# Unread products re-counted, the second tile's rows turned amid the first tile's products, a loaded table for the search, and a quarter of the map's slot columns made by ScalarE

## The chip, the cores and the metric

The kernel runs on one core of one Trainium2 chip. The metric is device time in microseconds (us) of that core. The core's engines run at the same time and meet at semaphores: TensorE (PE: matrix products, with its weight loads, PEld), VectorE (DVE), ScalarE (ACT), GpSimd (POOL, which here issues the indexed transfers) and SyncE (SP, which issues the plain ones); 16 DMA engines move data. All arithmetic here is in fp32, in which TensorE makes each product in two passes, so the profile counts two MATMULs for one call of `matmul` or `transpose`.

## What is computed

Two transformer layers on 4096 tokens (8 batches of 512) of width 256. Each has an attention and then a mixture of 8 experts; layer 0 gives every token to the expert with the highest affinity, layer 1 first lets each expert pick its CAP = 512 most probable tokens.

```python
def _L0_ffn_ref(input_features, centroids, ln_g, ln_b, w1, b1, w2, b2):
    aff = x @ centroids.T
    assign = jnp.argmax(aff, axis=1)
    ...
    for e in range(nE):
        h = _layernorm(xs, ln_g[e], ln_b[e])
        h = jax.nn.relu(h @ w1[e].T + b1[e])
        ye = xs + h @ w2[e].T + b2[e]
        y = y + jnp.where((es == e)[:, None], ye, 0.0)
...
def _L1_ffn_ref(x, Wg, W1, W2):
    probs = jax.nn.softmax(xt @ Wg, axis=-1)
    pT = probs.T
    _, top_idx = jax.lax.top_k(pT, cap)
    sel = jnp.zeros((E, T), dtype=bool).at[jnp.arange(E)[:, None], top_idx].set(True)
    masked = jnp.where(sel, pT, -jnp.inf)
    assigned = sel.any(axis=0)
    tok2exp = jnp.where(assigned, jnp.argmax(masked, axis=0), jnp.argmax(pT, axis=0))
    ...
    for e in range(E):
        gate = jnp.where(tok2exp == e, weights, 0.0)
        h = jax.nn.gelu(xt @ W1[e], approximate=False) @ W2[e]
        out = out + gate[:, None] * h
```

## The kernel before

The program has six stages, one after the other. Layer 0: attention; the plan (which token goes to which slot of which expert's tile); the experts. Layer 1: attention; search and plan; the experts. The order on every engine is the order in which the code is written, and each engine has its own function per stage; semaphores join them.

**The plan.** VectorE picks each token's expert (`choose`), TensorE counts with two products by constant matrices (`prefix_pe`), and VectorE works out each token's slot (`place`, `place_packed`). Then the map from tokens to slots is inverted (`invert_dve`, `invert_pe`). A slot number is split in the place within its tile (`low_f`) and the tile's first slot (`base_f`). For each of the 32 groups of 128 tokens there are 128 columns `low_hot` (is this token's place n?, 128 elements a partition), a row `tile_hot` (which tile?) and `held` = `tile_hot` times (token number, weight). TensorE multiplies `low_hot` by `held` and sums over the 32 groups in one bank (L1049, 64 MATMULs with 78 columns in layer 0 and 68 in layer 1). VectorE makes these operands in four parts of 8 groups (L1030, L1031, L1034) and tells TensorE after each (`p_low`). `keep_tokens` writes the result (L1056, L1057), and with it GpSimd fetches rows tile by tile with indexed transfers (L1173, L1899).

**Unread products.** `hold_clock(eng, n)` (L287) issues n products of the identity with itself into a bank that nobody reads. They stand where TensorE waits for others: 30 ahead of layer 0's map, 25 behind each map ahead of the experts' first rows, 34 ahead of layer 1's map.

**The experts, layer 0** (`expert_stage`, L1136). For each of 39 tiles of 128 rows: `turn_in` transposes the rows (L1198), ScalarE scales them (`act_in`, L1359), `up` makes the hidden layer (L1210, 32 MATMULs) with weights that VectorE has copied (`fetch_weights`, L1297 and L1303), ScalarE makes relu (L1365), `down` multiplies back (L1224), VectorE adds up (`out_rows`), GpSimd stores. There is one bank for turned rows, so `turn_in` of a tile waits until ScalarE has taken those of the tile before. In the steady order TensorE turns tile j, then does `up` of tile j - 1 and `down` of tile j - 2; tile 1 alone is turned behind `up` of tile 0. VectorE and ScalarE wait at the head of the stage for `s_bias`, the four loads that SyncE issues at L1075 to L1078.

**The experts, layer 1** (`f1_tensor` and its fellows, from L1907) have the same order with shorter products (L1916 turns, L1932 up, L1955 down); here too tile 1 is turned behind `up` of tile 0.

**The search** (from L2059) finds each expert's 512th largest probability as a bit pattern, in ROUNDS = 10 rounds of three bits. A round has seven candidates and zero: VectorE counts for the four odd ones how many keys reach them (L2093, with an accumulator read each), ScalarE does so for the three even ones with Sign (L2138) after it has scaled them (`under`, L2135), TensorE sums the counts over the partitions (L2154), and VectorE keeps the largest candidate that at least 512 keys reach (L2097, L2098) and makes the next candidates with the halved steps (L2090, L2095). The steps are built with memsets and shifts at the head of the stage.

## Time and profile before

| | us |
|---|---|
| median of 3 runs | 1015.35 |
| the 3 runs | 1011.42, 1015.35, 1015.40 |
| the profiled execution: its own time | 1017.07 |
| its span | 1015.1 |
| TensorE's mean granted clock, as a share of full speed | 0.975 |
| TensorE busy | 941.4 (93% of the span) |
| VectorE, ScalarE, GpSimd busy | 705.3, 491.7, 321.5 |

Where the stages lie in the span, read from TensorE's timeline: the plan of layer 0 from 205 to 224.7, its experts to 517.5, the attention of layer 1 to 795, search to 829.4, the plan of layer 1 to 861.7, its experts to the end. The times below are us from the span's start. The profiled execution's own time is 1.72 above the median and the three runs differ by 4, which is to be kept in mind where a sum from one trace is set beside the median. Matrix products are pipelined, so that a row's duration of the last one reaches over the next row's start: what a group costs is the distance between starts.

### The profile page before, as it was taken

The page shows a single profiled execution, that of the slowest core. Times are in us where ns is not written, and L with a number is a line of the kernel's source. Part 1 is how long each engine was busy: PE and PEld are TensorE (multiplying, and loading weights), DVE is VectorE, ACT ScalarE, POOL GpSimd, SP SyncE. Part 2 cuts the span into 40 slices and gives each one's busy share as a digit, 9 for nine tenths or more (in the row PEclk, how much of TensorE's full clock was granted, in tenths as well). Part 3 has the DMA queues.
Part 4 walks back from the last instruction along what each step waited for, and adds up shares of the span by engine and source line. Part 5 has one row for each costly group of instructions (what it writes and reads, how often), then busy time and mean ns, then how long its engine had stood idle before and what let it go on. Part 6 is the DMA issues. An engine that isn't in the chain of part 4 may idle for free. (4 is left out here: it accounts for less than half of the span.)

```text
span 1015.1 us, 29867 instructions
## 1 busy us (share of the span) xinstructions
PE 941.4 (93%) x11226; PEld 793.5 (78%) x11227; DVE 705.3 (69%) x1820; ACT 491.7 (48%) x1325; POOL 321.5 (32%) x288
## 2 busy tenths in 40 slices
PE   6899999987999999999999999999878889999996
PEld 3466666887999999999987778888767778888875
DVE  3567887873777777777640679899888777466662
ACT  3646565312545444454534868788762440222221
POOL 0034533612232323323120334434433000555562
PEclk9999999998999999999999999999999897999998
DMA  9884581285322223222116757766642710443440
GB/s 337 233 329 120 126 269 70 85 309 192 95 89 85 90 88 98 78 94 87 45 40 117 132 104 156 144 148 141 118 106 70 310 65 1 138 135 117 140 139 32
DMA packets 130474, 133.76 MB, mean 132 GB/s; under 512 B 73693, under 2 KB 118879, under 8 KB 128181
## 3 DMA queue, kind: packets, MB, share of 16 engines
q1 hardware_dynamic: 119764, 90.82, 32.3%
q0 software_dynamic: 10592, 41.30, 12.7%
q8 instruction: 82, 1.34, 0.6%
q14 instruction: 36, 0.29, 0.1%
HBM read 94.27 MB, written 44.11 MB: 136 GB/s over the span
## 5 line engine op out<-in xcount | busy, mean ns | idle before, releaser
L1210 PE MATMUL psall<-rows 128*128 128x128 f32 x1248 | 148.2, 278 | 1.7 <-DVE rows L1303 1.7
L1210 PEld LDWEIGHTS psall<-rows 128*128 128x128 f32 x1248 | 146.3, 195 | 2.9 <-ACT rows L1359 1.9
L1224 PE MATMUL psall<-whi,rows 128*128 x624 | 141.0, 379 | 0.0
L1224 PEld LDWEIGHTS psall<-whi,rows 128*128 128x128 f32 x624 | 115.7, 190 | 14.1
L1178 POOL DMA_INDIRECT attn_rows<-rows,tok_i x39 | 41.7, 1069 | 183.6 <-DVE rows L1335 183.6
L287 PE MATMUL psall<-cst 128*128 128x128 f32 x718 | 93.8, 289 | 0.6 <-PEq L1451 0.6
L1570 DVE STREAM_TRANSPOSE whi<-whi 32x512 f32<-32x512 f32 x128 | 89.9, 702 | 5.9 <-POOL whi L1529 3.8
L287 PEld LDWEIGHTS psall<-cst 128*128 128x128 f32 x718 | 89.5, 204 | 1.4 <-issue 1.1
L1303 DVE COPY rows<-wlo 128x2048 f32 (+1 forms) x39 | 47.3, 1214 | 58.1 <-PE psall L1210 49.4
L1365 ACT ACTIVATE rows<-psall,vs 128x128 f32<-128x128 f32 x312 | 84.6, 382 | 4.5 <-PE psall L1210 2.1
L1649 ACT ACTIVATE whi<-psall 32x512 f32<-32x512 f32 x128 | 75.1, 587 | 12.7 <-PE psall L1814 10.5
L1899 POOL DMA_INDIRECT x<-ffn_rows,tok_i x34 | 38.8, 1142 | 123.2 <-DVE tok_i L1057 74.3
L1741 PE MATMUL psall<-wlo,x 128*32 128x128 f32 x2048 | 65.6, 280 | 2.0 <-issue 1.9
L1741 PEld LDWEIGHTS psall<-wlo,x 128*32 128x32 f32 x2048 | 56.1, 113 | 12.0 <-issue 11.1
L1266 ACT ACTIVATE small<-small,eps_t 128x1 f32<-128x1 f32 x39 | 11.5, 295 | 107.0 <-DVE small L1330 107.0
L1529 POOL TENSOR_TENSOR whi<-whi,wlo 128x512 f32<-128x512 f32 x32 | 34.0, 1063 | 89.5 <-DVE wlo L1561 89.5
L773 PE MATMUL psall<-whi 128*128 128x512 f32 x128 | 58.0, 597 | 1.1 <-ACT key L679 1.1
L1173 POOL DMA_INDIRECT x<-ffn_rows,tok_i x39 | 40.0, 1025 | 52.8 <-issue 34.1
L1932 PE MATMUL psall<-rows 128*128 128x128 f32 x448 | 54.7, 275 | 0.5 <-ACT rows L1979 0.5
L1955 PE MATMUL psall<-wlo,rows 128*128 x224 | 54.0, 385 | 0.0
L1932 PEld LDWEIGHTS psall<-rows 128*128 128x128 f32 x448 | 52.3, 192 | 0.8 <-ACT rows L1979 0.8
L1979 ACT ACTIVATE rows<-psall 128x256 f32<-128x256 f32 x34 | 13.1, 385 | 78.1 <-PE psall L1916 78.1
(299 smaller groups left out, 1842.7 us busy)
## 6 DMA issues: line engine op xcount, KB each, us to landing
ffn_rows<-mod_rows SPq DMA_DIRECT2D x2, 4096.0 KB
wlo<-attn_rows SPq DMA_DIRECT2D x64, 128.0 KB, 3.3
wlo<-in_W SPq DMA_DIRECT2D x2, 4096.0 KB, 17.7
whi<-in_w SPq DMA_DIRECT2D x5, 1024.0 KB, 8.7
whi<-mod_rows SPq DMA_DIRECT2D x4, 1024.0 KB, 14.0
ffn_rows<-rows SPq DMA_DIRECT2D x8, 512.0 KB
ffn_rows<-x SPq DMA_DIRECT2D x8, 512.0 KB
v_turn<-wlo SPq DMA_DIRECT2D x32, 128.0 KB, 3.2
```

What stands on the lines that cost most here:

```text
L287: eng.matmul(b_idle, ident, ident, start=True, stop=True)
L773: last = eng.matmul(ps[k % 2][:, :], h0T[:, c, k * P:(k + 1) * P], wqkv[:, c, D:3 * D], start=c == 0, stop=c == C - 1)
L1178: eng.indirect_dma_start(dst_d, bass.IndirectOffsetOnAxis(tok_i[:, j:j + 1].bitcast(U32), 0), fout[j % 2], None, bounds_check=T - 1, oob_i ...
L1210: last = eng.matmul(b_up[t.par][f // 4][:, (f % 4) * P:(f % 4 + 1) * P], w_now[:, c, f * P:(f + 1) * P], inT[t.par][:, c * P:(c + 1) * P], ...
L1224: last = eng.matmul(b_dn[t.par][:, 0:D], hidT[t.par][:, f * P:(f + 1) * P], w_down[:, bass.ds(e, 1), f, :].rearrange("p o n -> p (o n)"), ...
L1303: eng.tensor_copy(w_now[:, :, part], w_of_e[:, :, part]).then_inc(e_["w"], 1)
L1365: last = eng.activation(dst[:, f * P:(f + 1) * P], banks[f // 4][:, (f % 4) * P:(f % 4 + 1) * P], ACT.Relu, bias=b1T[:, f, bass.ds(e, 1)])
L1570: last = eng.transpose(ebd[t % 2][rows_q, :, 32 * q:32 * q + 32], sc[t % 3][rows_q])
L1649: last = eng.activation(sc[t % 3][rows_q], b_s[rows_q, :, 32 * q:32 * q + 32], ACT.Copy)
L1741: last = eng.matmul(b_qk[t % 2][k * QD:(k + 1) * QD, n * P:(n + 1) * P], wqkv1[:, c, h * QD:(h + 1) * QD], hT[b % 2][:, c, k * P:(k + 1) * ...
L1932: last = eng.matmul(b_up1[t.par][:, f * P:(f + 1) * P], w_now1[t.full % 2][:, c, f * P:(f + 1) * P], inT1[t.par][:, c * P:(c + 1) * P], st ...
L1955: last = eng.matmul(b_dn1[t.par][:, 0:D], hidT1[t.par][:, f * P:(f + 1) * P], w_down1[:, bass.ds(e, 1), f, :].rearrange("p o n -> p (o n)" ...
```

## The change

1. **Unread products.** Ahead of layer 0's map 20 in place of 30, behind it 36 in place of 25, ahead of layer 1's map 33 in place of 34.
2. **Second tile.** In both layers tile 1's rows are turned in the middle of tile 0's `up`, not behind it.
3. **Waits.** In layer 0 VectorE waits for the bias loads only ahead of its first `out_rows`, not ahead of its first weight copy.
4. **The map's parts.** Six parts of 4, 4, 8, 8, 4 and 4 groups in place of four of 8. The slot columns of the third part are made by ScalarE: eight Square of (place - slot), then one Relu of 1 minus that.
5. **The search.** Steps, first candidates and bias come from a table of 128 x 129 words that SyncE loads at the head of the stage. VectorE makes all 88 combinations of eight outcomes and eleven next candidates while the counts are on their way, picks with one operation and one reduction, and ScalarE's scaling is folded in. Odd candidates count the keys below.

```diff
+def search_table():
+    n = np.array(ODD + EVEN + (0,) + EVEN, np.int64)
+    low = np.array((0,) * N_CAND + (1,) * len(EVEN), np.int64)
+    steps = np.concatenate([(n << (PROB_BITS - 3 * (i + 1))) - low for i in range(ROUNDS)]).astype(np.int32)
...
+        MAP_PARTS = ((0, 4), (4, 8), (8, 16), (16, 24), (24, 28), (28, 32))
+        BY_SCALAR = (8, 16)
...
-            ch.do(eng.tensor_copy(low_f, low_i))
+            eng.tensor_copy(low_f, low_i).then_inc(p_hot, 1)
+            eng.wait_ge(p_hot, 3 * layer + 1)
...
+            for lo, hi in MAP_PARTS:
...
+                if (lo, hi) != BY_SCALAR:
+                    eng.tensor_tensor(low_hot[:, part, :], bc_mid(count, n), bc_last(low_f[:, part], P), ALU.is_equal)
...
+        def map_scalar(eng, layer):
+            part = low_hot[:, slice(*BY_SCALAR), :].rearrange("p t n -> p (t n)")
+            eng.wait_ge(p_hot, 3 * layer + 1)
+            for t in range(*BY_SCALAR):
+                last = eng.activation(low_hot[:, t, :], count, ACT.Square, bias=low_f[:, t:t + 1], scale=-1.0)
+            last.then_inc(p_hot, 1)
+            eng.wait_ge(p_hot, 3 * layer + 2)
+            eng.activation(part, part, ACT.Relu, bias=ones[:, 0:1], scale=-1.0).then_inc(p_hot, 1)
...
-            hold_clock(eng, 30)
+            hold_clock(eng, 20)
...
-                hold_clock(eng, 25)
+                hold_clock(eng, 36)
...
                     for f in range(nf):
+                        if t.static and t.j == 0 and f == nf // 2:
+                            turn_in(Tile(0, 1))
...
                     eng.wait_ge(e_["dn"], t.j + 1)
+                    if not t.after(1):
+                        waits(eng, "out")
...
-            elif who in ("vector", "scalar"):
+            elif who == "vector":
+                eng.wait_ge(s_w1, 16)
+            elif who in ("scalar", "out"):
                 eng.wait_ge(s_bias, 64)
...
                     for f in range(NF1):
+                        if t.j == 0 and f == NF1 // 2:
+                            turn_in(Packed(1))
...
+                eng.dma_start(search, a["search"]).then_inc(s_cst, 16)
                 eng.dma_start(wlo[:, 0:8192], a["W1"]).then_inc(s_l1w, 16)
...
+                eng.wait_ge(s_cst, 32)
+                now = first
                 for i in range(ROUNDS):
-                    eng.tensor_tensor(cand, best.bitcast(I32).broadcast_to([P, N_CAND + len(EVEN)]), steps, ALU.bitwise_or).then_inc(q_cand, 1)
-                    eng.wait_ge(q_cand, i + 2)
+                    if i:
+                        now = cand
+                        eng.tensor_reduce(now, allowed, AX.X, ALU.max).then_inc(q_cand, 1)
+                        eng.wait_ge(q_cand, i + 1)
...
+                    if i < ROUNDS - 1:
+                        ch.do(eng.tensor_tensor(follow.bitcast(I32), bc_mid(now[:, 0:N_CAND].bitcast(I32), N_NEXT), bc_last(steps[i + 1], N_CAND), ALU.bitwise_or))
+                        ch.do(eng.tensor_scalar(follow[:, N_CAND:, :], follow[:, N_CAND:, :], LIFT, LOWEST, ALU.mult, ALU.max))
+                        eng.wait_ge(q_pe, pe_did("counts", i))
+                        ch.do(eng.scalar_tensor_tensor(allowed, bc_mid(ps[i % 2][:, 0:N_CAND], N_NEXT), few, follow, ALU.is_le, ALU.mult))
...
-                    eng.activation(under, cand_f[:, N_CAND:], ACT.Copy, scale=-LIFT).then_inc(q_act, 1)
-                    eng.wait_ge(q_act, act_did("under", i))
...
-                hold_clock(eng, 34)
+                hold_clock(eng, 33)
```

How the instructions stand on TensorE from layer 0's map to the second tile's `up` (L287 and L305 are `hold_clock`, L1049 and L1072 the map, L1198 and L1235 turn rows, L1210 and L1249 are `up`; a call counts once here). Before:

```order
L287 MATMUL psall<-cst 128x128 x25
L1198 MATMUL psall<-cst,x 128x128 [waits s_in0,p_tok]
L1198 MATMUL psall<-cst,x 128x128
L1210 MATMUL psall<-rows 128x128 [waits f0_w,f0_inT]
L1210 MATMUL psall<-rows 128x128 x15
L1198 MATMUL psall<-cst,x 128x128 [waits f0_inT,s_in1]
L1198 MATMUL psall<-cst,x 128x128
L1198 MATMUL psall<-cst,x 128x128 [waits f0_inT,s_in2]
L1198 MATMUL psall<-cst,x 128x128
L1210 MATMUL psall<-rows 128x128 [waits f0_w,f0_inT]
```

and after:

```order
L305 MATMUL psall<-cst 128x128 x36
L1235 MATMUL psall<-cst,x 128x128 [waits s_in0,p_tok]
L1235 MATMUL psall<-cst,x 128x128
L1249 MATMUL psall<-rows 128x128 [waits f0_w,f0_inT]
L1249 MATMUL psall<-rows 128x128 x7
L1235 MATMUL psall<-cst,x 128x128 [waits f0_inT,s_in1]
L1235 MATMUL psall<-cst,x 128x128
L1249 MATMUL psall<-rows 128x128 x8
L1235 MATMUL psall<-cst,x 128x128 [waits f0_inT,s_in2]
L1235 MATMUL psall<-cst,x 128x128
L1249 MATMUL psall<-rows 128x128 [waits f0_w,f0_inT]
```

The wait for ScalarE's second taking of rows (`f0_inT`, with `s_in1`) has moved from between the two tiles into the first tile's sixteen products.

VectorE in one round of the search (names as above; `q_pe` is TensorE's sum, `whi` holds all small arrays). Before:

```order
L2093 TENSOR_SCALAR whi<-whi 128x256 [waits q_cand]
L2093 TENSOR_SCALAR whi<-whi 128x256 x3
L2095 TENSOR_SCALAR whi<-whi 128x11
L2097 SCALAR_TENSOR_TENSOR whi<-psall,whi 128x8 [waits q_pe]
L2098 TENSOR_REDUCE whi<-whi 128x1 [waits s_vq]
L2090 TENSOR_TENSOR whi<-whi 128x11 [waits s_vq]
```

and after:

```order
L2125 TENSOR_SCALAR whi<-whi 128x256 [waits q_cand]
L2125 TENSOR_SCALAR whi<-whi 128x256 x3
L2128 TENSOR_TENSOR whi<-whi 128x88
L2129 TENSOR_SCALAR whi<-whi 128x24 [waits s_va]
L2131 SCALAR_TENSOR_TENSOR whi<-psall,whi 128x88 [waits q_pe,s_va]
L2122 TENSOR_REDUCE whi<-whi 128x11 [waits s_va]
```

Behind the sum stand two operations in place of three, and ahead of it two in place of one.

ScalarE between the search and layer 1's experts, after the change (L2175 is Sign, L1080 Square, L1083 Relu, L2017 takes turned rows, L2025 is Gelu):

```order
L2175 ACTIVATE whi<-whi 128x256 [waits q_cand]
L2175 ACTIVATE whi<-whi 128x256 x2
L1080 ACTIVATE rows<-cst,proj_bias 128x128 [waits p_hot,s_hst1,s_hst0]
L1080 ACTIVATE rows<-cst,proj_bias 128x128 x7
L1083 ACTIVATE rows<-rows,cst 128x1024 [waits p_hot]
L2017 ACTIVATE rows<-psall 128x256 [waits g_tin,p_tok]
L2017 ACTIVATE rows<-psall 128x256 [waits g_tin]
L2025 ACT_TABLE_LOAD
L2025 ACTIVATE rows<-psall 128x512 [waits g_up]
```

The nine new operations stand where ScalarE had none, with no load of a function table among them.

## Rows read from the trace of the kernel before

**Rows 1.** TensorE's timeline, layer 0's experts open: start, us, engine, line
```profile
222.66 2.01 PE L1049 MATMUL psall<-rows 128*128 128x78 f32 x16 [0.24 <-DVE rows L1034]
224.50 5.79 PE L287 MATMUL psall<-cst 128*128 128x128 f32 x50
233.09 0.41 PE L1198 MATMUL psall<-cst,x 128*128 128x128 f32 x2 [2.80 <-DMA x<-ffn_rows,tok_i]
235.23 6.22 PE L1210 MATMUL psall<-rows 128*128 128x128 f32 x32 [1.73 <-DVE rows L1303]
241.29 0.38 PE L1198 MATMUL psall<-cst,x 128*128 128x128 f32 x2
...
243.08 3.74 PE L1210 MATMUL psall<-rows 128*128 128x128 f32 x32
```
**Rows 2.** Busy time of five engines by stretch, then granted clock, DMA share, GB/s
```profile
238.00:240.00 2.00, 2.00 (x11) 2.00 (x11) 0.69 (x1) 0.00 (x0) 0.00 (x0) 0.50 0.00 0
...
852.00:854.00 2.00, 2.00 (x12) 2.00 (x11) 2.00 (x4) 0.00 (x0) 0.00 (x0) 0.50 0.00 0
```
**Rows 3.** Timeline of VectorE and ScalarE, the same opening
```profile
233.81 1.27 DVE L1303 COPY rows<-wlo 128x2048 f32 x1 [8.73 <-issue]
...
233.76 0.81 ACT L1359 ACTIVATE rows<-psall,vs 128x128 f32<-128x128 f32 x2 [24.17 <-PE psall L1198]
...
242.75 2.17 ACT L1365 ACTIVATE rows<-psall,vs 128x128 f32<-128x128 f32 x8
```
**Rows 4.** DMA issues, last us to landing: layer 0's first fetch, layer 1's, weights
```profile
x<-ffn_rows,tok_i POOLq DMA_INDIRECT x1, 6.6
...
x<-ffn_rows,tok_i POOLq DMA_INDIRECT x1, 4.5
...
wlo<-in_W SPq DMA_DIRECT2D x2, 4096.0 KB, 17.7
```
**Rows 5.** Timeline of the search: one round on three engines, and its last sum
```profile
799.27 0.43 PE L2150 MATMUL psall<-whi,cst 128*128 128x8 f32 x2
...
805.28 0.36 PE L2154 MATMUL psall<-whi,cst 128*128 128x8 f32 x2 [0.72 <-ACT whi L2138]
...
829.03 0.36 PE L2154 MATMUL psall<-whi,cst 128*128 128x8 f32 x2 [0.72 <-ACT whi L2138]
...
804.91 0.17 DVE L2095 TENSOR_SCALAR whi<-whi 128x11 int32<-128x11 int32 x1
805.68 0.17 DVE L2097 SCALAR_TENSOR_TENSOR whi<-psall,whi 128x8 f32<-128x8 f32 x1 [0.60 <-PE psall L2154]
...
806.28 0.48 DVE L2093 TENSOR_SCALAR_CACHE_REDUCE whi<-whi 128x256 f32<-128x256 f32 x1
...
803.55 0.51 ACT L2138 ACTIVATE whi<-whi 128x256 f32<-128x256 f32 x1
...
804.95 0.19 ACT L2138 ACTIVATION_READ_ACCUMULATOR whi<-whi 128x1 f32 x1
```
**Rows 6.** Timeline of layer 1's map and the opening of its experts
```profile
849.06 12.58 PE L1049 MATMUL psall<-rows 128*128 128x68 f32 x64 [0.92 <-DVE rows L1034]
...
868.74 0.38 PE L1916 MATMUL psall<-cst,x 128*128 128x128 f32 x2
869.66 2.05 PE L1932 MATMUL psall<-rows 128*128 128x128 f32 x16 [0.54 <-ACT rows L1979]
...
872.74 1.95 PE L1932 MATMUL psall<-rows 128*128 128x128 f32 x16
...
846.80 0.44 DVE L1030 TENSOR_TENSOR rows<-small,cst 128x272 f32<-128x272 f32 x1
847.15 1.22 DVE L1031 TENSOR_TENSOR rows<-cst,proj_bias 128x1024 f32<-128x1024 f32 x1
848.29 0.72 DVE L1034 TENSOR_TENSOR rows<-rows,token_weight 128x544 f32<-128x544 f32 x1
...
862.86 1.52 POOL L1899 DMA_INDIRECT x<-ffn_rows,tok_i  x1 [74.30 <-DVE tok_i L1057]
```

More of the change, by code:

```diff
@@ L46 @@
 SA, CA, GA, SB_, CB, GB = range(6)
+ODD, EVEN = (1, 3, 5, 7), (2, 4, 6)
+N_ODD, N_CAND, N_NEXT = 4, 8, 11
+ROUNDS = PROB_BITS // 3
+LIFT = 2.0 ** 64
+LOWEST = LIFT * 2.0 ** -127
+def search_table():
+    n = np.array(ODD + EVEN + (0,) + EVEN, np.int64)
+    low = np.array((0,) * N_CAND + (1,) * len(EVEN), np.int64)
+    steps = np.concatenate([(n << (PROB_BITS - 3 * (i + 1))) - low for i in range(ROUNDS)]).astype(np.int32)
+    first = steps[0:N_NEXT].view(np.float32).copy()
+    first[N_CAND:] *= np.float32(LIFT)
+    bias = np.array((0.0,) * N_ODD + (float(CAP) / (P // E),) * len(EVEN) + (0.0,), np.float32)
+    return np.tile(np.concatenate([steps, first.view(np.int32), bias.view(np.int32)]), (P, 1))
 def constants():
@@ L1058, in keep_tokens @@
             ch.sync()
-        p_one, p_pre, p_exp, p_low, p_inv, p_tok = (sem("p_" + n) for n in "one pre exp low inv tok".split())
+        p_one, p_pre, p_exp, p_low, p_inv, p_tok, p_hot = (sem("p_" + n) for n in "one pre exp low inv tok hot".split())
         cx = Carve(x)
@@ L1230, in turn_rest @@
                         turn_in(t)
[L1232 to L1235 removed]
+                pipeline(eng, [(ahead, turn_rest), (ahead + 1, up), (ahead + 2, down)], head)
             def on_scalar(eng):
@@ L1608, in _ @@
                 attn0_scalar(eng)
+                plan0_scalar(eng)
                 f0_scalar(eng)
@@ L1964, in step @@
                     up(second)
-                if now and now.j == 1:
-                    turn_in(now)
                 if fourth and fourth.mixed:
@@ L2131, in _ @@
                 eng.activation(keyE, ps[3][:, 0:2 * P], ACT.Copy).then_inc(q_act, 1)
+                eng.wait_ge(s_cst, 32)
                 for i in range(ROUNDS):
-                    eng.wait_ge(q_cand, i + 2)
-                    eng.activation(under, cand_f[:, N_CAND:], ACT.Copy, scale=-LIFT).then_inc(q_act, 1)
-                    eng.wait_ge(q_act, act_did("under", i))
+                    eng.wait_ge(q_cand, i + 1)
+                    now = cand if i else first
                     for n in range(len(EVEN)):
-                        last = eng.activation(signs[:, n, :], key_even, ACT.Sign, bias=under[:, n:n + 1], scale=LIFT, accum_out=parts[:, N_ODD + n:N_ODD + n + 1])
+                        last = eng.activation(signs[:, n, :], key_even, ACT.Sign, bias=now[:, N_CAND + n:N_CAND + n + 1], scale=-LIFT, accum_out=parts[:, N_ODD + n:N_ODD + n + 1])
                     last.then_inc(q_act, 1)
+                for i in range(2):
+                    eng.wait_ge(s_hst[i], 32 * NT // 2)
+                map_scalar(eng, 1)
                 f1_scalar(eng)
@@ L2212 @@
         "consts": constants(),
+        "search": search_table(),
     }
```

76 lines of the change are left out of this document (31 added, 45 removed).

## The prediction

> **What bounds the kernel now.** I read the timelines of the stages that the change touches first, then the granted clock by stretch, then the landing times of the transfers. TensorE works through both expert stages with no gap: once the second tile's `up` has begun, its rows follow one another, so a stage that opens earlier ends earlier by the same amount. Between these stages the work is a chain from engine to engine, and what a link there saves also moves the end. Five places matter.
>
> (a) Layer 0's opening. The unread products end at 230.3, the first rows land and are turned at 233.09, `up` of tile 0 starts at 235.23, tile 1 is turned at 241.29 and `up` of tile 1 starts at 243.08 [rows 1]. ScalarE takes tile 0's rows from 233.76 to 234.57, VectorE's weight copy runs from 233.81 to 235.08, and TensorE goes by the copy [rows 3]. The granted clock at 238 to 240 is 0.50, the level of 1.2 GHz [rows 2]; `up` of tile 0 therefore takes 6.06 from start to start, where the next one, at full speed, has a duration of 3.74 for the same 32 MATMULs, about 3.6 from start to start [rows 1].
>
> (b) The search. One round, sum to sum, is (829.03 - 805.28) / 8 = 2.97 [rows 5]. In it ScalarE is last: VectorE is free of its counts at 804.91 and its last read ends 0.08 later, ScalarE's last accumulator read ends at 805.14, and TensorE sums at 805.28.
>
> (c) Layer 1's map. VectorE starts it at 846.80 and a part of 8 groups costs it about 2.13; TensorE needs 12.58 for all 64 MATMULs and is at 0.50 clock from 852 to 854 [rows 2, 6]. Layer 0's map, at 78 columns, took 2.01 for 16, 0.125 each [rows 1]; at that speed this one would take 8.0. TensorE had stood 0.92 idle before it.
>
> (d) Behind the map, which ends at 861.64, 50 unread MATMULs fill the time to 868.74, 7.1 with none idle, against 5.79 in layer 0 [rows 1, 6]. GpSimd issues the first fetch at 862.86, it lands 4.5 later [rows 4, 6], at 867.4, so the unread products and not the fetch set 868.74.
>
> (e) Layer 1's opening: from the first turn at 868.74 to the second `up` at 872.74 are 4.00 [rows 6].
>
> **The change, part by part.**
>
> *Layer 0's map* gets smaller first parts. VectorE's costs scale from [rows 6]: about 0.07 an operation and 1.04 ns an element. With 78 columns, parts of 4 groups cost 1.23 and TensorE can start 1.1 earlier; the third part loses 1.13 on VectorE. The map ends about 1.1 earlier, and the first fetch is issued that much earlier. I cost this at nothing on the path: the fetch needs 6.6 to land here against 4.5 when alone [rows 4], so it is held up by the transfers issued before it (w2 and the four bias loads), and ScalarE must have the bias loads too. The range is 0 to 1.1.
>
> The Trainium skill ("DMA: Bandwidth & Descriptors", section "Queues, rings and completion order") says that each DMA engine takes turns among its queues packet by packet. By that rule the earlier fetch would gain a part of the 1.1, and the bias loads, which ScalarE waits for, would lose some. The landing time of the row stands between the two readings.
>
> *VectorE's wait for the bias loads* moves behind the copy. The copy then runs long before the rows land, and `up` of tile 0 starts when ScalarE is done, 234.57 + 0.17 = 234.74: 0.5 earlier. If the copy had not been last, it would be nothing.
>
> *36 unread products* (72 MATMULs at 0.116, from 5.79 / 50) end at 223.5 + 8.3 = 231.8, ahead of the landing, so they delay nobody at full clock. TensorE's idle time before `up` of tile 0 falls from 2.80 + 1.73 to about 1.3 + 1.2. I take it that the clock then stays at 2.4 GHz: gain 6.06 - 3.6 = 2.5. The other bound is 0.
>
> *Tile 1 turned amid tile 0's `up`*: between the two `up` stand 243.08 - 241.29 = 1.79 now. After, there are two pairs of transposes at about 0.23 each, one inside and one behind: 1.79 - 0.46 = 1.3. ScalarE has the half `up`, 1.8, for its 0.81, and VectorE's half copy has the same cover. Sum of layer 0's opening: 0.5 + 2.5 + 1.3 = 4.3.
>
> *The search.* Round 0 gains nothing: TensorE runs from 799.27 without a gap to its first sum, through 11 unread products that stay; memsets that go lie under that. In the nine other rounds ScalarE starts its first Sign with VectorE's first count, so TensorE sums at about 1.59 + 0.14 = 1.73 after the start by ScalarE, 1.74 to 1.80 by VectorE's four counts of 0.40 plus the read, in place of 1.97 (805.28 less 803.31, the round's start, one round ahead of 806.28). Then VectorE has 2 new operations from 1.60 on: 88 elements, 0.07 + 0.09 of work and about 0.25 to the end with its wait of 0.04, and 24 elements, 0.22: ready at 2.1, and the sum is readable at 1.78 + 0.40 = 2.18. So they just fit; were they 0.2 each longer, they would cost 0.3 a round. Behind the sum stand two operations of 88 elements, 0.28 each, in place of 0.20, 0.19 and 0.21 (805.68 to 806.28 is 0.60): 0.04 less. Together 0.19 + 0.04 = 0.23, times nine: 2.1. Range 0.5 to 2.4.
>
> *Layer 1's map.* With start 0 at VectorE's first L1030, parts of 4 groups cost 0.21 + 0.60 + 0.35 = 1.17, and TensorE starts at 1.3 in place of 2.26. The 66 unread MATMULs end at about 1.1, so the gap of 0.92 becomes 0.2. ScalarE's part: eight Squares, each between 0.26 (L1365: 2.17 for eight, from the product bank) and 0.50 (Sign, twice as wide) [rows 3, 5]; I take 0.31, near the first since the width is that of L1365, then Relu of 1024 elements at about 1.1 (L1031 has 1.22 on VectorE). They start 0.15 before 0 and are done at 3.6 (2.2 with room at 0.26, 5.1 at 0.50). VectorE's share of that part is ready at 3.6. So TensorE runs 1.3 to 2.3, 2.5 to 3.5, 3.7 to 5.7, 5.7 to 7.7 and on to 9.7: the map is done at 9.8 where it was at 861.64 - 846.80 = 14.8, if the clock stays up. That is 5.0, with the 2.1 of the search counted above.
>
> *Behind it* the same 50 unread MATMULs take 5.8 in place of 7.1 at full clock, and the first fetch, issued 1.2 and landing 5.7 after the map's end, is level with them: 1.3, less 0.1 for the fetch.
>
> *Layer 1's opening.* Up to the first `up` 0.92, `up` 1.9 (2.05 as a duration), two pairs of transposes 0.46: 3.3 in place of 4.00, 0.7. The second and third fetches, 1.5 to 1.8 apart, land just as they are asked for: I take off 0.2. Gelu's table load stands ahead of its wait and is covered. 0.5.
>
> Sum: 4.3 + 2.1 + 5.0 + 1.2 + 0.5 = 13.1. Against the profiled execution's own 1017.07 that gives 1004.0, against the median, 1.72 lower, 1002.3. I forecast **1003**, between the two.
>
> A rule against it: the Trainium skill ("ScalarE: Activation LUTs", section "Table sets: the hidden batching unit") lists relu and copy, but not square, among the functions that every set holds. A load would then come before Square and one back to Ln and Exp; the order of the changed program has none, so that rule does not bite. No run here shows the load's effect.
>
> **The rivals.**
>
> *The clock falls in layer 0's opening all the same.* TensorE's idle time is cut, not gone: 2.5 of 4.1. In the old map 0.92 idle amid sparse products was followed by 0.50 [rows 2, 6]. Price 2.5: 1005.5.
>
> *The clock falls in layer 1's map.* For: the products are as narrow as before, there are short waits ahead of each of the first three parts, and ScalarE may add 0.5 to one. Against: the gap of 0.92 goes, and in layer 0's map TensorE waited before every part (the last wait 0.24) and still needed only 0.125 a MATMUL [rows 1]. If it falls halfway, some 27 MATMULs cost 0.22 in place of 0.125 (12.58 / 64 is 0.197 with a fast start), 2.6, and the unread products behind run slow for a time, 2.0 to 2.3: price 4.8, 1007.8. With both, 1010.3.
>
> The Trainium skill ("TensorE: Matmul & The Clock Gate", section "A second HAM failure mode: psum-queue depth-cycling") says that small idle times between groups of matmuls, each turn anew, can make the clock swing. That is this rival, on six parts in place of four; layer 0's map before, with a wait ahead of every part, does not agree with it.
>
> *The runs behind the median did not have the slow map.* One of three was at 1011.42, 4 below the others, about what the slow map costs. If the median's run was fast there already, 6.2 of the sum shrinks to about 1.2: 1007 to 1008.
>
> *The table lands late, slower than before.* SyncE issues it just ahead of two loads of 4 MB that need 17.7 [rows 4]. All three other engines wait for it; TensorE wants it at 799.27, 4.0 after its issue at 795.3. Landing beyond that is lost one for one, for nothing else hides it. If it were held until the first large load has landed, at 813, it would cost 13.7 and all gains but the opening's go: 1017, and with a fallen clock 1021. Against: it is first in its queue and small, and fetches of 0.4 MB land in 4.5.
>
> **How the numbers follow.** Forecast case (both clocks hold) 0.42; clock falls in layer 0 only 0.20; in layer 1's map only, or a median that was fast there, 0.22; both 0.09; the table late or another wait 0.03; the rest, 0.04, is a better result than the sum, by the 1.1 of the earlier fetch. The likeliest gives 1003. The range takes in the first three and the bounds of the search and of the fetch: 1000 to 1009. A measurement of this kernel tells about 0.5% from no change, 5 us: faster is below 1010.3. Faster 0.89, same 0.08, slower 0.03.
>
> **What would show it.** In the trace after: `up` of tile 0 in about 3.8 (with two transposes within) and granted clock 1.00 around it, the second `up` 4.3 earlier; sums of the search 2.74 apart; layer 1's map in about 8.4 from first to last MATMUL, with clock 1.00, and 50 unread ones in 5.8; 3.3 from the first turn to the second `up`. The prediction is wrong if the third part waits for ScalarE by over 0.5, if the clock is 0.50 in either place, if the operations on 88 elements last over 0.4, or if the experts' stages do not carry an earlier opening to their end.

## The result and the profile after

| | before | after |
|---|---|---|
| median of the runs, us | 1015.38 (14 runs, 1009.03 to 1017.41) | 1009.92 (14 runs, 1004.77 to 1016.46) |
| ratio after / before, 95% interval | | 0.9946 (0.9924 to 0.9968) |
| profiled execution, its span | 1017.07, 1015.1 | 1010.23, 1008.2 |
| TensorE's mean granted clock | 0.975 | 0.979 |

The kernel is 0.5% faster, 5.5 us, where 12.4 were forecast: 1009.92 lies just above the range of 1000 to 1009. The 14 runs of after fall in groups, five from 1004.77 to 1006.17, eight from 1009.46 to 1011.69, and one at 1016.46; the profiled execution is of the second. The same instructions run at either clock level in different runs, so that a term is read below from the marks of its own stage. A kernel is judged by its median; where the runs of one fall in groups, the median jumps from one group to the other, and the means are given beside it.

Where the time went, from starts of rows on TensorE (us from the span's start; ends of a map are its last row's):

| mark | before | after | gain of the stretch | forecast |
|---|---|---|---|---|
| layer 0's map ends | 224.67 | 228.12 | -3.45 | 0 |
| first turn, layer 0 | 233.09 | 237.66 | -1.12 | 0 |
| second `up`, layer 0 | 243.08 | 246.96 | +0.69 | 4.3 |
| experts of layer 0 end | 517.52 | 521.48 | -0.08 | 0 |
| search starts | 795.30 | 795.44 | +3.82 | 0 |
| last sum of the search | 829.03 | 828.22 | +0.95 | 2.1 |
| layer 1's map ends | 861.64 | 855.75 | +5.08 | 5.0 |
| first turn, layer 1 | 868.74 | 862.26 | +0.59 | 1.2 |
| second `up`, layer 1 | 872.74 | 865.77 | +0.49 | 0.5 |

Layer 0 is 3.9 late at its second `up` where it should have been 4.3 early; layer 1 does nearly what was forecast. The 3.82 between them is layer 1's attention, which the change does not touch; it comes back to this below.

TensorE's timeline of layer 0, as [rows 1], of the kernel after (start, us, engine, line, idle time before and what ended it):

```profile
209.14 4.63 PE L305 MATMUL psall<-cst 128*128 128x128 f32 x40
215.18 12.94 PE L1072 MATMUL psall<-rows 128*128 128x78 f32 x64 [1.42 <-DVE rows L1055]
227.91 9.90 PE L305 MATMUL psall<-cst 128*128 128x128 f32 x72
237.66 0.38 PE L1235 MATMUL psall<-cst,x 128*128 128x128 f32 x2
240.23 2.54 PE L1249 MATMUL psall<-rows 128*128 128x128 f32 x16 [2.19 <-ACT rows L1396]
242.57 0.63 PE L1235 MATMUL psall<-cst,x 128*128 128x128 f32 x2
243.00 2.93 PE L1249 MATMUL psall<-rows 128*128 128x128 f32 x16
245.76 0.38 PE L1235 MATMUL psall<-cst,x 128*128 128x128 f32 x2
246.96 3.25 PE L1249 MATMUL psall<-rows 128*128 128x128 f32 x27 [0.82 <-DVE rows L1338]
```

Busy time by stretch of the kernel after, the granted clock third from the end, as [rows 2]:

```profile
218.00:220.00 2.00, 2.00 (x11) 2.00 (x11) 2.00 (x4) 0.00 (x0) 0.00 (x0) 0.50 1.10 464
224.00:226.00 2.00, 2.00 (x12) 2.00 (x11) 0.00 (x0) 0.00 (x0) 0.00 (x0) 0.50 0.97 418
...
242.00:244.00 2.00, 2.00 (x11) 2.00 (x11) 0.69 (x1) 0.58 (x2) 0.00 (x0) 0.50 0.00 0
850.00:852.00 2.00, 2.00 (x20) 2.00 (x20) 2.00 (x5) 0.00 (x0) 0.00 (x0) 1.00 0.00 0
```

The story is in the first two rows. Forty unread MATMULs end at 213.8, VectorE is done with the first part only at 215.1, TensorE stands 1.42, and from 217.7 to 231.4 it is granted 0.50, the level of 1.2 GHz: the 64 MATMULs of the map take 12.94, where those of before took 8.75 (215.92 to 224.67). The map itself starts 0.74 earlier (1.0, reckoned from the counting products ahead, which are 0.28 late in this trace), near the 1.1 forecast. The unread products behind it end at 237.8, the first turn follows without a wait for the rows, and so these products now set it. Then `up` of tile 1 waits 0.82 for VectorE's copy (L1338), and the clock is at 0.50 here as well, at 242 to 244.

VectorE's and ScalarE's timeline of the same opening, as [rows 3]:

```profile
229.47 1.23 DVE L1338 COPY rows<-wlo 128x2048 f32 x1 [0.94 <-issue]
242.97 0.69 DVE L1332 COPY rows<-wlo 128x1024 f32 x1 [12.27 <-PE psall L1249]
246.12 0.69 DVE L1338 COPY rows<-wlo 128x1024 f32 x1 [2.45 <-PE psall L1249]
...
239.37 0.81 ACT L1396 ACTIVATE rows<-psall,vs 128x128 f32<-128x128 f32 x2 [22.10 <-PE psall L1235]
```

The first copy has left the path, from 233.81 to 229.47. The second weight set is copied in two halves, and the second half (L1338, 246.12) cannot start until `up` of tile 0 is over; `up` of tile 1 waits for both halves before its first product.

The search, as [rows 5] (VectorE L2128, L2129, L2131 and L2122 are the four new operations):

```profile
825.41 0.39 PE L2195 MATMUL psall<-whi,cst 128*128 128x8 f32 x2 [0.53 <-DVE whi L2125]
...
828.22 0.39 PE L2195 MATMUL psall<-whi,cst 128*128 128x8 f32 x2 [0.53 <-DVE whi L2125]
...
825.27 0.24 DVE L2128 TENSOR_TENSOR whi<-whi 128x88 int32<-128x88 int32 x1
825.55 0.18 DVE L2129 TENSOR_SCALAR whi<-whi 128x24 f32<-128x24 f32 x1
825.90 0.25 DVE L2131 SCALAR_TENSOR_TENSOR whi<-psall,whi 128x88 f32<-128x88 f32 x1 [0.17 <-PE psall L2195]
826.19 0.24 DVE L2122 TENSOR_REDUCE whi<-whi 128x11 f32<-128x88 f32 x1
```

A round is 2.80 where it was 2.97 (803.05 for the first sum, 828.22 for the tenth). Its last link is now VectorE's four counts, no longer ScalarE. The search's DMA issue of the table, and the map and opening of layer 1, as [rows 4] and [rows 6]:

```profile
whi<-in_search SPq DMA_DIRECT2D x1, 64.5 KB, 1.8
```

```profile
839.97 8.68 PE L305 MATMUL psall<-cst 128*128 128x128 f32 x66
848.49 7.26 PE L1072 MATMUL psall<-rows 128*128 128x68 f32 x64
855.59 5.80 PE L305 MATMUL psall<-cst 128*128 128x128 f32 x50
862.26 0.41 PE L1954 MATMUL psall<-cst,x 128*128 128x128 f32 x2 [0.88 <-DMA x<-ffn_rows,tok_i]
...
865.77 1.95 PE L1972 MATMUL psall<-rows 128*128 128x128 f32 x16
...
846.07 2.44 ACT L1080 ACTIVATE rows<-cst,proj_bias 128x128 f32<-128x128 f32 x8 [18.01 <-DVE proj_bias L1043]
848.54 1.15 ACT L1083 ACTIVATE rows<-rows,cst 128x1024 f32<-128x1024 f32 x1
```

The table lands in 1.8. Layer 1's map has no wait ahead of it, since the unread products (slowed for a time by a low clock at 839 to 842.4) end only at 848.6, and no wait within: 7.26 at full clock in place of 12.58. ScalarE's Squares cost 0.31 each, as taken. Behind it the first turn waits 0.88 for the fetch, and the fetch is late because of VectorE (VectorE's and GpSimd's timeline):

```profile
854.11 0.14 DVE L1025 TENSOR_SCALAR extra<-extra 128x1 f32<-128x1 f32 x1
...
856.62 0.19 DVE L1089 COPY slot_w<-psall 128x34 f32<-128x34 f32 x1
...
857.73 1.53 POOL L1937 DMA_INDIRECT x<-ffn_rows,tok_i  x1 [69.04 <-DVE tok_i L1090]
```

The map's last row ends at 855.75, but VectorE is in the work that it does behind its last part (ten operations from 854.11 to 856.59, which tell each tile its expert), so it takes the map only at 856.62. In the kernel before, the same work was over 3.9 before the map's end.

### The profile page after: what moved, and what is told of

The parts are those of the page before. It is cut to its first block and busy times, and to the rows that moved or that the text cites. A ratio compares the mean times of both kernels' runs of the same rounds, so it can differ in the third digit from the quotient of the medians.

```text
span 1008.2 us, 29881 instructions
## 1 busy us (share of the span) xinstructions
PE 940.8 (93%) x11226; PEld 791.9 (79%) x11227; DVE 705.2 (70%) x1811; ACT 497.1 (49%) x1333; POOL 323.4 (32%) x288
## 5 line engine op out<-in xcount | busy, mean ns | idle before, releaser
L1249 PE MATMUL psall<-rows 128*128 128x128 f32 x1248 | 147.5, 277 | 3.0 <-ACT rows L1396 2.2
L1249 PEld LDWEIGHTS psall<-rows 128*128 128x128 f32 x1248 | 145.5, 193 | 4.4 <-ACT rows L1396 2.4
L305 PE MATMUL psall<-cst 128*128 128x128 f32 x718 | 95.4, 292 | 1.0 <-PEq L1488 1.0
L305 PEld LDWEIGHTS psall<-cst 128*128 128x128 f32 x718 | 91.0, 207 | 2.1 <-issue 1.6
L1338 DVE COPY rows<-wlo 128x2048 f32 (+1 forms) x39 | 47.4, 1216 | 48.9 <-PE psall L1249 45.1
L1687 ACT ACTIVATE whi<-psall 32x512 f32<-32x512 f32 x128 | 75.2, 587 | 12.4 <-PE psall L1852 10.2
L1210 POOL DMA_INDIRECT x<-ffn_rows,tok_i x39 | 40.9, 1047 | 56.5 <-issue 36.2
L1995 PEld LDWEIGHTS psall<-wlo,rows 128*128 128x128 f32 x224 | 40.4, 190 | 11.9 <-issue 7.5
```

The costliest lines, as they stand in the source:

```text
L305: eng.matmul(b_idle, ident, ident, start=True, stop=True)
L1249: last = eng.matmul(b_up[t.par][f // 4][:, (f % 4) * P:(f % 4 + 1) * P], w_now[:, c, f * P:(f + 1) * P], inT[t.par][:, c * P:(c + 1) * P], ...
L1338: eng.tensor_copy(w_now[:, :, part], w_of_e[:, :, part]).then_inc(e_["w"], 1)
L1687: last = eng.activation(sc[t % 3][rows_q], b_s[rows_q, :, 32 * q:32 * q + 32], ACT.Copy)
L1995: last = eng.matmul(b_dn1[t.par][:, 0:D], hidT1[t.par][:, f * P:(f + 1) * P], w_down1[:, bass.ds(e, 1), f, :].rearrange("p o n -> p (o n)" ...
```

## The experiments

The variants ran in three sets, each beside runs of the kernel before: gap10, fill25, fill25_25 and before_fill38 beside a median of 1014.83 (23 runs); old_search25, turn_behind25, all_vector25 and best1 beside 1015.86 (20 runs); half_copy25, best1_old and best2 beside 1013.15 (15 runs). Differences between sets carry this difference too. "25" in a name means that the kernel has 25 unread products ahead of layer 0's map.

| kernel | median, us (runs) | ratio to before (95%) |
|---|---|---|
| after, in a set of its own | 1009.92 (14) | 0.9946 (0.9924 to 0.9968) |
| gap10 | 1009.48 (12) | 0.9946 (0.9919 to 0.9974) |
| fill25 | 1003.84 (6) | 0.9907 (0.9877 to 0.9938) |
| fill25_25 | 1007.75 (10) | 0.9936 (0.9914 to 0.9958) |
| before_fill38 | 1007.78 (8) | 0.9932 (0.9905 to 0.9958) |
| old_search25 | 1007.74 (8) | 0.9924 (0.9893 to 0.9955) |
| turn_behind25 | 1005.15 (7) | 0.9908 (0.9875 to 0.9942) |
| all_vector25 | 1010.44 (12) | 0.9946 (0.9919 to 0.9972) |
| half_copy25 | 1002.88 (6) | 0.9896 (0.9870 to 0.9923) |
| best1 | 1002.10 (7) | 0.9885 (0.9851 to 0.9919) |
| best1_old | 1006.23 (10) | 0.9930 (0.9906 to 0.9955) |
| best2 | 1003.35 (6) | 0.9900 (0.9874 to 0.9927) |

**The gap ahead of layer 0's map.** My theory: TensorE's idle 1.42 there brings the lower clock. The rival: the smaller parts with their waits do it, whatever stands ahead.

```diff
-            hold_clock(eng, 20)
+            hold_clock(eng, 25)     fill25
+            hold_clock(eng, 10)     gap10
```

> The changed kernel with 25 unread products in place of 20 ahead of layer 0's map, nothing else. In its trace 40 MATMULs end at 213.8 and the map starts at 215.18, 1.42 idle; the map then takes 12.94 with the granted clock at 0.50 from 217.73. Theory (the idle time ahead of the map lets the clock fall amid it): 50 MATMULs end at 214.9, 0.2 idle, the map takes about 8.5 at clock 1.00, the unread products behind it 8.4 in place of 9.9, and the runs all lie with the changed kernel's faster group (1004.8 to 1006.2), median 1005.5. Rival (the clock falls for another reason, such as the shorter waits within the map or the opening of the experts): the map still takes 12 to 13 in the trace and the median stays at 1009 to 1011.

> The changed kernel with 10 unread products in place of 20 ahead of layer 0's map. Theory: 20 MATMULs end at 211.5, 3.7 idle ahead of the map, so the clock is low in the map in every run: no run at 1005, median 1010.5 to 1012. Rival (idle time there does not matter): the same two groups as the changed kernel, median 1009.9, some runs at 1005.

TensorE's timeline of fill25:

```profile
209.05 6.51 PE L305 MATMUL psall<-cst 128*128 128x128 f32 x50
215.41 3.90 PE L1072 MATMUL psall<-rows 128*128 128x78 f32 x32
219.54 3.80 PE L1072 MATMUL psall<-rows 128*128 128x78 f32 x32 [0.24 <-DVE rows L1055]
...
233.36 0.41 PE L1235 MATMUL psall<-cst,x 128*128 128x128 f32 x2 [1.94 <-issue]
234.93 3.48 PE L1249 MATMUL psall<-rows 128*128 128x128 f32 x16 [1.16 <-ACT rows L1396]
...
241.46 3.81 PE L1249 MATMUL psall<-rows 128*128 128x128 f32 x32 [0.82 <-DVE rows L1338]
```

and of gap10:

```profile
214.92 13.77 PE L1072 MATMUL psall<-rows 128*128 128x78 f32 x64 [2.15 <-DVE rows L1055]
```

Five unread products more, with the same six parts, and the map takes 7.93 in place of 12.94; the first turn is at 233.36 in place of 237.66. The median falls by 6.1, the mean by 4.6 (1009.15 to 1004.52); against gap10, which ran beside it, the mean falls by 5.1. With ten fewer than in after the gap is 2.15 and the map takes 13.77, at the lower clock from 215.1 to 232.2. One trace each would prove little where the clock varies from run to run, but nine kernels have the 25, and in eight of their nine traces this map is at full clock throughout; the ninth is all_vector25, with a gap of another origin, below. So it is the gap and not the parts. What missed is the size of gap10: its median is that of after, and two of its runs, at 1001.74 and 1004.47, are as fast as fill25's; a gap of 2.15 makes the fall no more certain than one of 1.42. The earlier map also gained nothing at the first turn, 233.36 against 233.09 of before, as forecast. This trace names no releaser for it; in those of turn_behind25 and best1 it is the fetch.

**The unread products behind that map.**

```diff
-                hold_clock(eng, 36)
+                hold_clock(eng, 25)     fill25_25
```

> As fill25, and 25 in place of 36 unread products behind layer 0's map, as the kernel before has. Theory of the prediction (the longer row holds the clock for the opening of the experts, 2.5 us): tile 0's 32 MATMULs of up at clock 0.50, about 6.2, and a median 2 to 2.5 above fill25. Rival (the clock falls there with 36 too, or holds with 25): the same as fill25 within 0.5.

3.9 above fill25. In its trace the first turn waits 4.45 for the fetch and the second `up` is at 244.69, 9.78 behind the first turn, where fill25 has 8.10. So the 36 are worth 1.7 in the trace, 3.0 by the means and 3.9 by the medians. They do not hold the clock to the end: in fill25's trace it is low from 234.6 to 238.0, and the first half of `up` takes 3.48 in the row above in place of 2.05.

**The gap ahead of layer 1's map, in the kernel before.** If the clock is the whole matter there, four unread products in the old kernel do the work of the smaller parts and of ScalarE's share.

```diff
-                hold_clock(eng, 34)
+                hold_clock(eng, 38)     before_fill38
```

> The kernel before with 38 unread products in place of 34 ahead of layer 1's map, nothing else. Its trace has 0.92 idle there, then the map takes 12.58 with the clock at 0.50. Theory: 8 more MATMULs fill the 0.92; the map takes 8.4, the unread products behind it 5.8, the median falls by 4 to 5 us to 1010.5 to 1011.5. Rival (the products of 68 columns are too sparse in themselves to keep the clock): the map still takes over 11 and the median stays at 1015.

TensorE's timeline of before_fill38:

```profile
840.01 8.64 PE L287 MATMUL psall<-cst 128*128 128x128 f32 x76
848.68 8.37 PE L1049 MATMUL psall<-rows 128*128 128x68 f32 x64
856.89 5.80 PE L287 MATMUL psall<-cst 128*128 128x128 f32 x50
863.09 0.41 PE L1916 MATMUL psall<-cst,x 128*128 128x128 f32 x2 [0.41 <-issue]
```

The map takes 8.37 in place of 12.58 and the unread products behind it 5.80 in place of 7.1: 5.6 at the first turn (868.74 to 863.09; 5.3, reckoned from the first unread product, 840.39 and 840.01), and 7 by the medians. Four unread products in the old kernel bring at least what the whole change did (5.5; the intervals overlap), and of the 5.1 that the change gained up to this map's end 4.2 could be had by the clock alone.

**ScalarE's quarter.** VectorE makes all slot columns again; the parts and the 25 stay.

```diff
-                if (lo, hi) != BY_SCALAR:
+                if True:
                     eng.tensor_tensor(low_hot[:, part, :], bc_mid(count, n), bc_last(low_f[:, part], P), ALU.is_equal)
...
-                if (lo, hi) == BY_SCALAR:
-                    eng.wait_ge(p_hot, 3 * layer + 3)
...
-                map_scalar(eng, 1)
```

> As fill25, with the slot columns of the third part made by VectorE too (six parts, ScalarE makes none). VectorE's part costs 1.13 more in each map. Theory (in layer 0 the first fetch lands no earlier for an earlier map, in layer 1 the whole stage moves and short waits in the map grow to 1 us ahead of the third part, so that the clock falls in some runs): layer 0 no difference, layer 1 map ends 0.9 to 1.1 later at full clock, median 1 to 2 above fill25, 1005 to 1006. Rival (the ScalarE part is worth nothing, since TensorE is the slower one in layer 1's map): within 0.4 of fill25.

TensorE's timeline of all_vector25, both maps:

```profile
215.03 2.35 PE L1070 MATMUL psall<-rows 128*128 128x78 f32 x16 [0.30 <-DVE rows L1055]
218.51 9.36 PE L1070 MATMUL psall<-rows 128*128 128x78 f32 x48 [1.13 <-DVE rows L1055]
...
847.75 1.90 PE L1070 MATMUL psall<-rows 128*128 128x68 f32 x16
850.32 9.38 PE L1070 MATMUL psall<-rows 128*128 128x68 f32 x48 [0.67 <-DVE rows L1055]
```

1010.44, 6.6 above fill25 (5.0 by the means) where 1 to 2 were expected. The third part, whose slot columns VectorE must make again, comes late, and TensorE waits 1.13 and 0.67 ahead of it. The clock falls to 0.50 1.6 and 1.3 behind the start of the 48 MATMULs that are left, and is low from 220.1 to 230.4 and from 851.6 to 861.8. I had priced ScalarE's share by the work that it takes from VectorE; what it does is close two waits. The Trainium skill ("TensorE: Matmul & The Clock Gate", section "A second HAM failure mode: psum-queue depth-cycling") says that small idle times between groups of matmuls can make the clock swing. The traces here agree in that gaps of 0.67 to 2.15 ahead of narrow products were followed by the lower level, once in a map and not to and fro, while waits of 0.19 to 0.30 (fill25, best1) did no harm.

**Tile 1 turned amid `up`, and the half copy.**

```diff
-                        if t.static and t.j == 0 and f == nf // 2:
-                            turn_in(Tile(0, 1))       turn_behind25 (and the same in layer 1)
...
-                    eng.wait_ge(e_["w"], t.j + (2 if t.after(1) else 1))
+                    eng.wait_ge(e_["w"], 2 if t.static and t.j == 1 else t.j + (2 if t.after(1) else 1))     half_copy25
```

> As fill25, with tile 1's rows turned behind tile 0's up in both layers, as the kernel before does. Prediction: 1.3 + 0.5, so 1.8 slower than fill25, 1005.6. Theory from fill25's trace (in layer 0 the second up waits for VectorE's copy of the second half of the weights, 0.82 idle, which starts only when the first up has ended, so the turn amid it gains only about 0.4 there; in layer 1 0.6): 1.0 slower, about 1004.9.

> The kernel with 25 unread products ahead of layer 0's map (fill25), and one wait changed: `up` of tile 1 in layer 0 starts when VectorE has copied the first half of its weights, not both. Theory (turning tile 1 amid `up` gained only some 0.4 us of its 1.3 in layer 0 because `up` of tile 1 stands for VectorE's second half copy, 0.82 in the trace of the changed kernel): no wait for that copy any more, 7.3 from the first turn to the second `up` where fill25 has 8.1, and 0.8 off the time at best, about 1003.0 for fill25's 1003.8; so small a step is read from the trace, not from the medians. Rival (the wait only hides another: ScalarE's taking of the rows, or the clock): the second `up` starts as late as in fill25.

turn_behind25 is 1.3 above fill25 where 1.0 was expected, though intervals of 0.3% do not tell 1.3 from nothing (the means differ by 0.2). In layer 1 its trace has 4.03 from the first turn to the second `up` and fill25's 3.41. In layer 0 there are 1.79 between the two `up` (241.21 to 243.00), the same as before, and in fill25 1.21 (240.25 to 241.46, with the transposes within, another 0.2): the turn amid `up` gained 0.4. With the wait for the second half gone, half_copy25 shows the rest (TensorE's timeline):

```profile
233.45 0.41 PE L1235 MATMUL psall<-cst,x 128*128 128x128 f32 x2 [1.90 <-issue]
235.02 2.69 PE L1249 MATMUL psall<-rows 128*128 128x128 f32 x16 [1.16 <-ACT rows L1396]
237.50 0.63 PE L1235 MATMUL psall<-cst,x 128*128 128x128 f32 x2
237.93 2.78 PE L1249 MATMUL psall<-rows 128*128 128x128 f32 x16
240.54 0.38 PE L1235 MATMUL psall<-cst,x 128*128 128x128 f32 x2
240.76 3.74 PE L1249 MATMUL psall<-rows 128*128 128x128 f32 x32
```

7.31 from the first turn to the second `up`, to the number expected, though the clock is still low from 236.2 to 239.7.

**The search.**

```diff
-                        eng.tensor_reduce(now, allowed, AX.X, ALU.max).then_inc(q_cand, 1)
+                    eng.tensor_tensor(cand, best.bitcast(I32).broadcast_to([P, N_CAND + len(EVEN)]), steps, ALU.bitwise_or).then_inc(q_cand, 1)
...     the rest of the search of the kernel before: old_search25 (in fill25), best1_old (in best1)
```

> As fill25 (the changed kernel with 25 unread products ahead of layer 0's map), with the search of the kernel before: steps built with memsets and shifts, no table, ScalarE scales the even candidates. It tells what the search part is worth. In the changed kernel's trace the sums of two rounds stand 2.81 apart, before 2.97, and the first sum is not earlier. Theory: median 1.4 to 1.5 above fill25's 1003.84, about 1005.3, and 2.97 between sums. Rival (the prediction's 2.1 is right and the trace understates it): 1006. Rival (the table's load costs something elsewhere): no difference.

> The best version so far (best1: 25 unread products ahead of layer 0's map, the half copy, 42 behind that map, 5 between the first turn and the first `up`, 27 ahead of layer 1's second counting products) with the search of the kernel before. It prices the new search where the clock is kept in both maps. Theory (the new search is worth what its rounds save, 0.16 in each of nine, 1.4 us, plus at most 0.5 at its head): 1003.5 to 1004 against best1's 1002.1, and both maps at full clock. Rival (its worth is larger, through the clock in layer 1's map, as the 3.9 us between old_search25 and fill25 seem to say): 1006, with the granted clock at 0.50 in or ahead of layer 1's map.

By the medians both missed in the same way: 3.9 above fill25 and 4.1 above best1, against the 1.5 that the rounds account for (in best1_old's trace the sums are 2.97 apart again, 9 x 0.17 = 1.5, and both maps run at full clock, 8.50 and 8.18). The rival's clock in layer 1's map is not there either. In best1_old's trace the clock is low from 859.0 to 862.4, in the opening of layer 1, and the second `up` comes 4.57 after the first turn in place of 3.54. That is 1.0 more, in one execution. The other 1.5 or so no trace shows. Old_search25's runs fall in two groups (three from 1003.68 to 1004.79, five from 1007.17 to 1008.62); its mean is 2.2 above fill25's, and the two ratios differ by 0.17%, so that its miss is within the noise. Best1 and best1_old ran in different sets; best2, which has the new search and ran beside best1_old, is 2.9 below it. What the search is worth beyond 1.5 stays open.

**A better version.** best1 is half_copy25 with 42 in place of 36 behind layer 0's map, 5 unread products between the first turn and the first `up`, and 27 in place of 18 ahead of layer 1's second counting products, where TensorE stood 1.97 in the trace after. best2 takes some away at the head of the search.

```diff
-                hold_clock(eng, 36)
+                hold_clock(eng, 42)
...
+                    if t.static and t.j == 0:
+                        hold_clock(eng, 5)
...
-                hold_clock(eng, 18)
+                hold_clock(eng, 27)
```

> As fill25, with: the second up of layer 0 starting on the half copy of the weights (it waits for the rest in its middle, where a wait stands already), 42 in place of 36 unread products behind layer 0's map, 5 more between the first turn and the first up, and 27 in place of 18 ahead of layer 1's second counting products, which fill 2 us of idle time. Theory: 0.8 for the half copy, 1.5 for the clock of the first up, 0.5 for the clock ahead of layer 1's map: 1001 median. Rival (the clock is not kept, or the longer rows of unread products delay the turn): within 0.5 of fill25 or above it.

> best1 with 5 unread products in place of 8 at the head of the search and 9 in place of 11 ahead of its first sum. In best1's trace TensorE's transposes stand 0.7 behind the keys that they turn, and the first sum some 0.5 behind the counts, both times for unread products. Theory (what ends those waits last is the unread products): the search's first sum 1.0 earlier against the search's start, 1001.1 for best1's 1002.1. Rival (fewer unread products there bring the lower clock, as fewer did ahead of layer 0's map): the granted clock is 0.50 in the rounds of the search or behind it, and nothing is gained, 1002 to 1005.

TensorE's timeline of best1, layer 0's opening:

```profile
222.86 9.59 PE L305 MATMUL psall<-cst 128*128 128x128 f32 x84
232.71 0.41 PE L1235 MATMUL psall<-cst,x 128*128 128x128 f32 x2 [0.26 <-DMA x<-ffn_rows,tok_i]
232.96 1.28 PE L305 MATMUL psall<-cst 128*128 128x128 f32 x10
234.25 2.05 PE L1251 MATMUL psall<-rows 128*128 128x128 f32 x16
...
238.36 3.74 PE L1251 MATMUL psall<-rows 128*128 128x128 f32 x32
```

Here the clock holds, and from the first turn to the second `up` it is 5.65 where before had 9.99: 4.34 gained, the 4.3 of the forecast. This is the trace of best1's fastest run, 997.80 against 1001.37 for the next. The clock holds in the opening of best2 and best1_old too, which have the same products, but there the stretch is 6.80 and 6.50, since ScalarE takes the rows 1.83 and 1.53 after the turn and not 0.68. Best1's median of 1002.10 is 1.15% below before's, 13.8 us, and about where the forecast put the change itself. In best2 the first sum should have come 1.0 earlier. It comes 7.44 after the head's start (789.56 to 797.00) where best1 has 7.09, since the clock is low from 787.9 to 798.1, for 10.2, where in best1 it is low for 6.8 (783.4 to 790.2); the median is 1.25 above best1's, less than these runs can tell. The stretch begins ahead of the edit in both, so the trace speaks for the rival, that these products help the clock back, without settling it.

## Why the prediction was wrong

**Layer 0's map was the step that failed.** It was costed at nothing, with its range of 0 to 1.1 above nothing, because the fetch sets the first turn. That much holds: in turn_behind25 the map ends at 223.40, 1.27 earlier than before, and the first turn is at 233.12 for 233.09. But the step moved only VectorE's end of the wait. The unread products ahead of the map fell from 30 to 20, which takes 10 x 0.23 = 2.3 off TensorE's side against 1.1 on VectorE's: a gap of 0.2 + 1.2 = 1.4 was there to be worked out from the rows, and it is 1.42. The same prediction priced a gap of 0.92 as the cause of 0.50 clock in layer 1's map [rows 2, 6] and never asked the question of layer 0's. It cost 4.6 at the first turn in the trace, and 6.1 by the medians of fill25 and after, 4.6 by their means.

**Layer 0's opening, 4.3.** It gave 0.69 in after. 0.5 for the copy behind the bias wait: the copy went to 229.47 as said, and in fill25 `up` of tile 0 comes 1.57 behind the first turn in place of 2.14, 0.57 less. In after it came 2.57 behind, since ScalarE took the rows 1.71 after the first turn (237.66 to 239.37) and not 0.67 as before; gap10 has 1.61. What holds ScalarE there stays open. It is not the bias loads, the last of which landed at 232.3 in after (issued at 219.85, 12.4 to landing), nor the late turn, for all_vector25, with its turn at 237.04, has 0.62, while best2, with its turn at 233.56, has 1.83. 2.5 for the clock: from its start to tile 2's turn, with one pair of transposes within, `up` of tile 0 takes 5.53 in after and 5.32 in fill25, both partly at 0.50, and 3.89 in gap10, all_vector25 and best1, all at 1.00. So 0.7 of the 2.5 came and 1.6 failed, 1.4 in fill25. The count of 36 does not decide it: gap10 and all_vector25 have no more than after and hold the clock there, behind a map that ran at 0.50 until 232.2 and 230.4, while fill25, half_copy25, turn_behind25 and old_search25, with the same 36, do not; with 42 and five more behind the turn it held in all three traces. Which of these two additions keeps it was not tested. In the rival's price, TensorE's idle time was put at "2.5 of 4.1"; by the rows it was 2.80 + 1.73 = 4.53. 1.3 for the turn amid `up`: 0.4, because the wait for the second half copy, "the same cover" in the prediction, has no cover at all: the copy starts only behind the `up` that should have hidden it. Half_copy25 got another 0.8.

**The search, 2.1.** The nine rounds gave 0.17 each, 1.5, in place of 0.23; the head lost 0.57 in this trace (its first sum comes 7.61 after the first unread product, 7.04 before, with the clock low to 801.4), and 0.95 is left. The loss at the head is the clock of this one execution and not the change's: in fill25, with the same head, the first sum comes after 7.04 again. Ahead of the sum the step was right: 1.75 from the round's start (826.47 to 828.22) in place of 1.97, 0.22 for the 0.19 taken, with VectorE last. Behind it failed the term of 0.04: the two operations take 0.57 in place of 0.60, but the first begins 0.49 after the sum (825.41 to 825.90) where it began 0.40 after it, "readable at 0.40" in the sum; so 0.06 is lost and not 0.04 gained.

**Layer 1's map, 5.0 to its end.** It gave 5.08, though most of it by a way that I had put as a condition, "if the clock stays up": before_fill38 got 4.2 of it with four unread products. That the sum agrees to 0.1 is luck in part: the map does not start earlier (10.33 behind the counting products, 10.11 before), since the low clock kept the unread products ahead of it until 848.6, and for this it found all its parts ready and took 7.26, not 8.4. ScalarE's Squares and Relu were sized right (0.31, 1.15). **Behind it**, 1.2: 0.59 came. The fetch was to be issued 1.2 behind the map's end, as before; it is issued 1.98 behind (857.73 less 855.75), since VectorE, now overtaken by TensorE, is busy to 856.6. The prediction left this work of VectorE out. In fill25 and best1 VectorE takes the map 0.92 behind its end as well. **The opening**, 0.5: 0.49.

**What hid the miss.** Layer 1's attention took 277.8 before and 274.0 after, with the same instructions. Across the kernels it took from 271.3 (turn_behind25) to 278.1 (old_search25), with 15 and 26 us at the lower clock; that time alone does not give the order, since after has 10 and before 18. Of the 6.9 that the two profiled spans differ, 3.8 are of this kind and owe nothing to the change, while layer 0's loss of 3.9 is of the change. The sum by stages is then 3.1 for the change in this one execution, and 5.5 by the medians: some executions of after, those near 1005, may have run layer 0's map at full clock, as the 4 to 5 us between its groups suggest. No trace of one of them was taken, so this is argued and not shown.

Of the rivals, "the clock falls in layer 0's opening" came true, at 1.6 for its 2.5. The clock in layer 1's map held, and the table landed in 1.8.

## What to carry to other kernels

Products that nobody reads are counted for one wait; when a change moves either end of that wait, count them anew from both ends, with the wait's end less the products' end as the number to look at. A gap of one microsecond among narrow products can cost four behind it, and so four unread products can be worth as much as a rebuilt stage: try them first, alone. When work is to hide a transfer or a copy, look at what that copy itself waits for before you take its cover as given.

## What the runs showed of the hardware

The thirteen traces hold 26 maps. In five of them TensorE stood idle by 0.67 us or more ahead of a group of map products of 68 or 78 columns: 0.67 and 1.13 (all_vector25), 0.92 (before), 1.42 (after) and 2.15 (gap10). Each of the five was followed by 0.50 granted clock, which began 0.2 to 2.6 us behind the gap and stayed past the map's end, up to 17 us in all (gap10). In the other 21, with waits of at most 0.30, the map is at full clock. Gaps are not the whole of it: the lower clock comes elsewhere too, as in the 10 to 26 us of it in layer 1's attention, and with the same gap the medians of after and gap10 stand over runs up to 8 us faster, of which there is no trace.

A fetch that is issued sooner need not land sooner. Turn_behind25 issues its first fetch at 225.08 where before does so at 226.33; it needs 7.9 to land in place of 6.6, and the first turn is at 233.12 for 233.09. Some 0.8 of this lies in GpSimd, whose issuing instruction takes 1.98 in place of 1.20. The Trainium skill ("DMA: Bandwidth & Descriptors", section "Queues, rings and completion order") says that the DMA engines take turns among their queues packet by packet, by which a sooner issue would have gained a part; the landing shows nothing of it in this place.
